# Accumulating three key-pair sums in a row into one gather buffer instead of alternating between two

## The reference

```python
scores = jnp.einsum('bhqd,bhkd->bhqk', q, k) / math.sqrt(dk)
scores = jnp.where(causal[None, None], scores, -jnp.inf)
attn = jax.nn.softmax(scores, axis=-1)
ctx = jnp.einsum('bhqk,bhkd->bhqd', attn, v)
```

## Time and profile before

| | us |
|---|---|
| median of 3 runs (1587.35 to 1590.1) | 1588.08 |
| the profiled execution | 1589.09 |
| its span in the profile | 1587.4 |

### The profile page before, as it was taken

The page is one execution under the profiler, slowest core; times in us unless marked ns, Lnnn a source line. Parts: engine busy times, 40 slices in busy tenths (PEclk is TensorE's granted clock), DMA queues, the critical chain, the costliest instruction groups (busy, mean ns, idle before and its releaser), DMA issues.

```text
span 1587.4 us, 24844 instructions
## 1 busy us (share of the span) xinstructions
PE 1545.5 (97%) x9088; PEld 971.1 (61%) x9088; DVE 1147.6 (72%) x2273; ACT 767.6 (48%) x1540; POOL 884.5 (56%) x593
## 2 busy tenths in 40 slices
PE   7999999979999999999999999999999999999999
PEld 5888887644555555555555555555555536777777
DVE  6766666858777777777777777777777767666665
ACT  3222222234666666666665665666666673223221
POOL 2332323245787788787787787787877822111111
PEclk9999999979999999999999999999999999999999
DMA  5555785493367368358359449448435364222321
GB/s 199 205 206 179 225 275 182 147 196 68 86 140 174 81 133 187 81 124 196 81 114 196 92 99 199 97 94 192 102 88 127 83 147 137 80 80 82 134 78 53
DMA packets 120399, 215.83 MB, mean 136 GB/s; under 512 B 12502, under 2 KB 45782, under 8 KB 113110
## 3 DMA queue, kind: packets, MB, share of 16 engines
q1 hardware_dynamic: 102380, 136.20, 31.8%
q0 software_dynamic: 8064, 58.72, 18.0%
q10 hardware_dynamic: 9840, 19.40, 3.4%
HBM read 96.23 MB, written 58.72 MB: 98 GB/s over the span
## 4 chain that ended last, share of the span: by engine, by line
PE 90%; DVE 5%; DMA 2%; issue 1%; ACT 1%; SPq 1%; POOL 0%; DVEq 0%; POOLq 0%; ACTq 0%
PE a_mx L230 20%; PE a_av L975 16%; PE a_st L962 15%; PE p_pair L466 11%; PE f_wo_ps L1312 6%; PE p_v L478 5%; PE f_out_ps L1372 5%; PE a_sum L995 2%; DVE a_part L245 2%; PE a_sum L1003 2%; PE f_mid_ps L1312 1%; PE f_lg_ps L1342 1%; PE f_out_ps L1387 1%; PE a_mx L234 1%; PE p_tr L446 1%
## 5 line engine op out<-in xcount | busy, mean ns | idle before, releaser
L1056 ACT ACTIVATE a_probs<-a_st 128x512 f32<-128x512 f32 (+2 forms) x1244 | 584.3, 536 | 375.7 <-PE a_st L962 367.5
L245 DVE TENSOR_REDUCE a_part<-a_mx 128x1 f32<-128x512 f32 (+2 forms) x842 | 538.2, 681 | 117.3 <-PE a_mx L230 100.5
L915 POOL TENSOR_TENSOR a_pair<-a_probs 128x1024 f32<-128x1024 f32 (+2 forms) x224 | 397.8, 1801 | 39.3 <-ACT a_probs L1056 15.3
L230 PE MATMUL a_mx<-a_k_stack,a_q_stack 96*128 96x512 f32 (+3 forms) x640 | 243.1, 405 | 1.6 <-DVE a_part L245 0.5
L915 POOL TENSOR_TENSOR a_gather<-a_probs 128x1024 f32<-128x1024 f32 x76 | 179.4, 2381 | 112.8 <-ACT a_probs L1056 112.8
L230 PEld LDWEIGHTS a_mx<-a_k_stack,a_q_stack 96*128 96x128 f32 x640 | 117.6, 190 | 164.3 <-DVE a_part L245 122.7
L248 DVE CUSTOM_DVE_ANT_0 a_mx<-a_mx,f_ctx 128x384 f32<-128x384 f32 (+1 forms) x240 | 148.8, 632 | 86.7 <-PE a_mx L230 86.7
L962 PE MATMUL a_st<-a_q_stack,a_k_stack 98*128 98x512 f32 (+2 forms) x604 | 209.8, 367 | 1.4 <-DMA a_q_stack<-a_neg_rows 1.4
L362 POOL TENSOR_TENSOR p_rot<-p_mul 128x1024 f32<-128x1024 f32 x32 | 89.9, 2810 | 204.9 <-DVE p_mul L644 204.9
L1305 POOL TENSOR_TENSOR f_x<-f_x,f_bias 128x512 f32<-128x512 f32 x32 | 41.5, 1327 | 205.1 <-DVE f_xn L1522 205.1
L975 PE MATMUL a_av<-a_probs,a_v 128*32 128x512 f32 (+3 forms) x1280 | 150.5, 543 | 1.7 <-POOL a_probs L896 1.7
(11 more groups left out here) (195 smaller groups left out, 2415.5 us busy)
## 6 DMA issues: line engine op xcount, KB each, us to landing
a_gather<-a_pair POOLq DMA_DIRECT2D x56, 1024.0 KB, 7.2
a_k_stack<-qk_scratch SPq DMA_DIRECT2D x72, 256.0 KB, 8.3
qk_scratch<-p_rot_hi SPq DMA_DIRECT2D x32, 512.0 KB, 3.1
qk_scratch<-p_rot_lo SPq DMA_DIRECT2D x32, 512.0 KB, 3.9
a_q_first<-qk_scratch SPq DMA_DIRECT2D x48, 256.0 KB, 6.5
a_q_stack<-qk_scratch SPq DMA_DIRECT2D x48, 256.0 KB, 4.9
v_scratch<-p_v_st SPq DMA_DIRECT2D x32, 256.0 KB, 7.3
ctx_scratch<-a_ctx_st SPq DMA_DIRECT2D x32, 256.0 KB, 2.6
```

The source lines that it names most:

```text
L230: mm = pe.matmul(places[:, i, :], queries[0:96, head, qi * P:(qi + 1) * P], keys[0:96, head, 0:width], start=(i == 0), stop=not masked_her ...
L245: dve.tensor_reduce(found, scores.rearrange("p (h n) -> p h n", n=width), AX.X, ALU.max).then_inc(self.max_done, 1)
L915: pool.tensor_tensor(place[:, h:h + 2, q0:TT], probs[:, s % RING, h:h + 2, q0:TT], probs[:, (s + 1) % RING, h:h + 2, q0:TT], ALU.add).then ...
L1056: act.activation(probs[:, s % RING, h, q0:TT], score_bank(g, HG * s + h)[:, q0:TT], ACT.Exp, scale=SCORE_SCALE).then_inc(exp_done, 1)
```

## The change

It alters two tables. Unit 2's full pairs all go to buffer 0: pair 6 directly, pairs 7, 8 and 9 by joins, each of which waits for the one before. Unit 2's only gather sum is at pair 11. Unit 3's pairs swap buffers: pair 12 goes to buffer 1 and pair 13 to buffer 0 directly, joins 14 and 16 to buffer 1, joins 15 and 17 to buffer 0; pair 18 sums buffer 1 and pair 19 buffer 0. Unit 1 is unchanged. As pair 10 no longer has a gathered sum, `plan_items` spreads the items a little differently.

```diff
-    return (1, n == 0) if t == 1 else (n % 2, n < 2)
+    return (2 - t, n == 0) if t < 3 else ((n + 1) % 2, n < 2)
 
...
-GATHERED_SUMS = {}
-for _t in range(1, QT):
-    GATHERED_SUMS[LAST_PAIR[_t]] = 1
-    if _t > 1:
-        GATHERED_SUMS[LAST_PAIR[_t] - 1] = 0
+GATHERED_SUMS = {LAST_PAIR[1]: 1, LAST_PAIR[2]: 0, LAST_PAIR[3] - 1: 1, LAST_PAIR[3]: 0}
```

## The result

The changed kernel takes 1628.22 us (median of 4 runs, 1625.58 to 1639.87) against 1589.09 us for the kernel before in the same comparison: 1.0258 times as long, 95% interval 1.0205 to 1.0311. The forecast was 1583.1 with a range up to 1589.5: the time is far outside the range and moved the other way. The profiled execution took 1625.58 us, its span is 1623.8.

The account below looks back on a forecast made before the run. PE, busy 97% of the span, was taken as the bound: -5.95 us for gather sums, +1.0 for one long landing, 0 for the last group, -4.95 in all, from 1588.08 to 1583.1 us; range 1580.0 to 1589.5.

Parts of the forecast that it names:

- Bound, and the worth of PE time: Attention stage, groups 0 to 6: PE idles only 0.6 to 0.9 us per group, so PE time saved shortens the kernel.
- The 0.85 per group: PE at pair 10: dropping one gather-sum batch saves 0.85 us in each of seven groups, 5.95 us.
- Removed and added work: PE loses eight L995 records per group (320 to 256); POOL gains one join, about 0.9 us, not a bound by volume.
- Landings: Joins 7 and 8 of unit 2 land in 7.1 and 6.9 us, sum 14.0; one 8.4 landing costs 1.0 us.
- The rival with long landings: Serial joins 7 and 8 hold join 9, delaying pair 10's masks and sum; slower from 15.2 us, 1593.3 to 1597.3; chance 0.12.
- The serial chain: POOL, joins 7 to 9 then pair 10's sum: PE stalls only if both landings exceed 14.35 us; hand-overs 0.04.
- the 0.35 to spare: Pair 10's sum on POOL: likeliest landings of joins 7 and 8 total 14.0, 0.35 us under the stall limit.
- The 1.1 us of cover for the masks of step 20: Masks of pair 10 behind join 9 on POOL: end near 656.0, PE's product on them starts at 657.10.
- Later waits, costed at nothing: Behind join 9: masks of step 20 and pair 11's sums stay covered, the latter by over 2 us; cost nothing.
- Sharing the DMA engines: Store of unit 1's context beside join 7: skill's rate lengthens the join by 0.6 us; the trace row shows 0.2.
- The planner's share, taken as nothing: Single maxima items shift between pairs: bounds 2.5 us won or as much lost over seven groups, taken as nothing.
- The last group: Head group 7: PE waits 1.45 us for unit 3's shift rows, so no gain; taken as 0, bounds -0.6 and +1.5.

Follow-up runs that it names:

- the best version: Changed kernel, join 9 behind pair 10's masks and sum, query load two steps later, old tables in last group, pair 11 summed in buffer 1, PE's buffer-0 sum later: 1582.53 us.
- a quarter of join 9: Changed kernel with join 9 transferring one head of four (256 KB instead of 1 MiB), leaving three heads of pair 9 out of the denominators: 1595.5 us.
- the run with the one moved join: Kernel before, with only join 9 issued behind pair 10's masks, some 3 us later; buffers, sums and items kept: 1629.73 us, ratio 1.0249.
- the later-load run: Changed kernel with SP's load of the next group's unit 2 queries issued two steps of scores later: 1604.88 us, ratio 1.0102.

## Why the prediction was wrong, point by point

- *Bound, and the worth of PE time.* Right: in the best version, 1582.53 us, a full group takes 0.95 us less than before on average (121.73 against 122.67), 0.7 of it less busy time on PE. The 0.85 per group was to be had.
- *Removed and added work.* Right: 256 gather-sum records instead of 320, 64 joins instead of 56.
- *Landings.* Right: join 7 lands in 7.1 to 7.3 us (one 8.7), join 8 in 6.8 to 6.9 (one 7.5), against 7.1 and 6.9. The rival with long landings was the cause in group 1 alone: 8.7 + 6.9 = 15.6 is over its limit of 15.2, the mask of pair 10 came 1.7 us late and the clock fell behind it. In the other full groups the sum is 14.0 to 14.6.
- *The serial chain.* Mis-sized by 1 us. I gave two hand-overs 0.04 us in all. In group 3 join 7 lands 7.1 us after 775.27 and join 8 is issued at 782.95; join 8 lands 6.9 us after that and join 9 goes at 790.35: more than 0.5 us each time, and so in every group. From join 7 to the end of pair 10's sum it is 20.87 us against 19.84 worked out, and the 0.35 to spare became a wait of 0.97. The 1.1 us of cover for the masks of step 20 went with it. This term alone would have eaten the gain: 122.77 us in a typical group with a quarter of join 9, against 122.6 before.
- *Later waits, costed at nothing.* The step that failed. I asked what is queued behind join 9 on POOL and who reads what it writes, and not what else is in flight on the DMA engines while it runs. Unit 3's rows are, in every group, and step 24 needs them. Where the prediction had nothing, the runs showed 13.3 us of waits for them (1.4 before), nearly all at step 24, and the 1.2 GHz level behind five of these pauses; delaying join 9 alone, in the kernel before, gave 1629.7 us. Their issue stood in the trace of the kernel before (655.52, 2.8 us behind join 9 in group 2). The prediction names the rows, as a shared wait, only in the last group. Pair 11's gather sum had the cover I gave it.
- *Sharing the DMA engines.* I weighed what the Trainium skill ("DMA: Bandwidth & Descriptors", "Issuing engines are not separate DMA queues") says on sharing 16 engines against the wrong victim, the join. The same page of the Trainium skill (section "Queues, rings and completion order") has each engine alternate between queues packet by packet. As I read it, the small rows would then pass quickly beside a join. The trace disagrees in effect: where PE waited for rows issued within about 1.5 us of a join, step 24 started 7.7 to 9.5 us after their issue.
- *The planner's share, taken as nothing.* Wrong by far: 1628 against 1599 us. Not through DVE or PE, as feared, but because one item fewer in pair 10 lets SP's query load start 0.6 us earlier, in among the held-back rows; moving that load alone gives 23 of these 29 us back.
- *The clock.* Not in the prediction at all, and worth an estimated 20 of the 35 us between the gather sums, which together with the pauses (22) more than eat the 6.9 saved.
- *The last group.* 75.4 against 71.8 us up to 2 us behind the last gather sum, outside the bound of +1.5. The prediction asked there only when pair 10's sum comes, and not its masks: PE waits 2.5 us for one, while its wait for the rows is as before (1.47 and 1.45). A late pair sum of DVE adds another 1.8 us (0.3 before); the best version has it too, with the old tables in this group, so it isn't the joins' doing. Join 9 serial behind join 8 alone gives +3.2.

## What to carry to other kernels

When a large transfer moves in time, list every transfer that is in flight beside it, small ones first, and who waits for those; program order on the issuing engine shows only half of what is behind it. A stretch that is 99.5% busy on PE has no cover for a pause: price a pause of 2 us by what the clock does after it, too, and not by its length alone. And where removed work should give a gain and the time doesn't show it, look for the arrivals that moved. Here the gain came out (0.44%) once the transfer, the small rows and the query load were kept apart, the last group had its old tables, and pair 11's sum no longer waited for join 9.

## What the runs showed of the hardware

- A join of 1 MiB, issued from POOL, held most of the small packets of SP's queue until its data were through, some 6.5 us after its issue. With a join of 256 KB the rows were there in time, at the latest 7.0 us after its issue. Why the engines serve them so is not shown.
- From the landing of a join that POOL waits for to POOL's next join it takes 0.5 to 0.6 us.
- Pauses of PE of 1.7 to 2.1 us, in groups 1 to 6 of the changed kernel and of the run with the one moved join, were each followed by the 1.2 GHz level, for 3 to 14 us: twelve of twelve. In the changed kernel a pause of 0.9 to 1.0 us stands some 3 us ahead of five of them. In the last group of the run with join 9 behind join 8, pauses of 2.1 and 2.5 us were not followed by it. After pauses of 1.5 us and less the clock mostly stayed at 2.4 GHz, though not always: in one group of the later-load run it fell after pauses of 1.0 and 0.4 us. What decides on a given occasion stays open.
